# A token model's attention loop: values in tiles of 32 queries, masks in 16 tiles, another order of tasks

## What is computed

```python
Q, K, V = (split_heads(x @ w) for w in (wq, wk, wv))            # 16 heads of 16
local = local_window_attn(Q, K, V)                              # blocks of 64 queries, each sees its block and the one before
GQ = split_heads(x @ wgq)                                       # 8 latent heads of 16
GK, GV = pool_to_latents(x @ wgk), pool_to_latents(x @ wgv)     # 64 latents
lsc = where(latent <= token // chunk, GQ @ GK.T / 4, -inf)
rem = softmax(lsc) @ GV @ r_out_w
gl, gr = sigmoid(Q . gate_local_w), sigmoid(Q . gate_remote_w)
h = h + (gl * local + gr * rem) @ w_out                         # x is the layer norm of h
# then: balanced assignment of all tokens to 8 experts, layer norm, gelu MLP, residual
```

## Time and profile before

| | |
|---|---|
| median of 3 runs | 3000.45 us (2997.2 to 3000.47) |
| profiled execution | 3003.33 us, span 3001.5 us |
| TensorE matmuls busy | 2668.5 us (89%) |
| VectorE busy | 1795.5 us (60%) |
| ScalarE busy | 1091.1 us (36%) |
| GpSimd busy | 752.9 us (25%) |
| granted TensorE clock, mean | 0.971 |

### The profile page before, as it was taken

The page is one execution under the profiler, slowest core; times in us unless marked ns, Lnnn a source line. Parts: engine busy times, 40 slices in busy tenths (PEclk is TensorE's granted clock), DMA queues, the critical chain, the costliest instruction groups (busy, mean ns, idle before and its releaser), DMA issues. The chain is left out here.

```text
span 3001.5 us, 83138 instructions
## 1 busy us (share of the span) xinstructions
PE 2668.5 (89%) x32904; PEld 1793.9 (60%) x32904; DVE 1795.5 (60%) x5503; ACT 1091.1 (36%) x1898; POOL 752.9 (25%) x998
## 2 busy tenths in 40 slices
PE   2899899899999899899899994299999999999998
PEld 1566666666666566566666663166656565666666
DVE  4556556556556556566566556775767667675720
ACT  0343343343343343433333431143333434343343
POOL 1011111121121121121121100134444453434543
PEclk9999999999999999999999998599999999999999
DMA  2000000010010010010000001001020211101020
GB/s 71 11 23 24 17 24 23 17 28 18 17 28 18 18 29 16 19 28 16 21 26 16 23 9 45 15 29 59 30 64 28 65 46 49 64 28 61 30 67 29
DMA packets 51568, 93.71 MB, mean 31 GB/s; under 512 B 7980, under 2 KB 36728, under 8 KB 51096
## 3 DMA queue, kind: packets, MB, share of 16 engines
q0 software_dynamic: 18432, 50.36, 5.9%
q1 hardware_dynamic: 32792, 38.52, 3.9%
HBM read 55.29 MB, written 33.55 MB: 30 GB/s over the span
## 5 line engine op out<-in xcount | busy, mean ns | idle before, releaser
L985 PE MATMUL S_ps<-hT,w 128*128 128x512 f32 x1024 | 478.4, 614 | 15.1 <-ACT hT L694 12.1
L998 PE MATMUL O_ps<-w,hid 128*128 128x256 f32 x2048 | 460.3, 379 | 0.0
L496 POOL DMA_INDIRECT rows<-in_tok_table,idx_now x128 | 129.4, 1011 | 1171.5 <-PE M_ps L883 928.0
L998 PEld LDWEIGHTS O_ps<-w,hid 128*128 128x128 f32 x2048 | 383.0, 190 | 62.5 <-issue 15.3
L1096 DVE TENSOR_REDUCE mxL<-S_ps 128x16 f32<-128x2048 f32 x128 | 293.0, 2289 | 155.8 <-PE S_ps L804 155.8
L632 ACT ACTIVATE PT<-S_ps 128x2048 f32<-128x2048 f32 x128 | 240.3, 1878 | 279.0 <-PE S_ps L772 279.0
L705 ACT ACTIVATE hid<-S_ps,b 128x512 f32<-128x512 f32 x256 | 175.3, 687 | 425.4 <-PE S_ps L985 408.5
L985 PEld LDWEIGHTS S_ps<-hT,w 128*128 128x128 f32 x1024 | 190.0, 194 | 223.5 <-issue 212.1
L828 PEld LDWEIGHTS O_ps<-bdV,PT 128*64 128x64 f32 x7680 | 249.2, 138 | 53.4 <-issue 47.5
L665 ACT ACTIVATE bdV<-M_ps 64x256 f32<-64x256 f32 x256 | 98.8, 386 | 490.7 <-PE M_ps L900 489.2
L828 PE MATMUL O_ps<-bdV,PT 128*64 128x34 f32 x7680 | 263.6, 225 | 1.9 <-DVE loc L1112 1.9
(11 more groups left out here) (237 smaller groups left out, 4248.5 us busy)
## 6 DMA issues: line engine op xcount, KB each, us to landing
h_rows<-h SPq DMA_DIRECT2D x64, 256.0 KB, 2.1
w<-in_w SPq DMA_DIRECT2D x16, 1024.0 KB, 5.9
rows<-in_tok_table,idx_now POOLq DMA_INDIRECT x128, 3.5
out_rows<-orow,idx_cur POOLq DMA_INDIRECT x128, 2.4
PT<-in_tables SPq DMA_DIRECT2D x1, 1024.0 KB
b<-in_b SPq DMA_DIRECT2D x8, 128.0 KB, 4.9
hrow<-h_rows,idx_next POOLq DMA_INDIRECT x64
hrow<-h_rows,idx_cur POOLq DMA_INDIRECT x64
```

The costliest lines, as they stand in the source:

```text
L985: mm = nc.tensor.matmul(S_ps[:, m % 2, 0:GT * P], w1[:, c, m * P:(m + 1) * P], hT[g % 2][:, c, :], start=c == 0, stop=c == KC - 1)
L998: mm = nc.tensor.matmul(O_ps[:, q % 2, 0:D], hid[:, m, q * P:(q + 1) * P], w2[:, m, :], start=m == 0, stop=m == FC - 1)
```

## The change

There are four parts. The values: `pe_values` cuts 64 queries in two halves of 32, so that a weight tile is 128 keys by 32 queries and writes one of four quarters of the partitions of `O_ps`. The masks of S 0 to 5: `pe_small_masks` takes 16 tiles of 32x32, each once, in place of eight matmuls in four tiles of 64x64; the tables are held in two or four rotated copies for it, and are larger in the load and in setup. The masks of S 6 to 9 stay. The order: the four `V` are spread over the rounds S 5 to S 7, `ET` moves to the round of S 8 one iteration sooner (relative sequence 2), the splitting of `mxR` becomes a task of its own (`SPLR`), and `GET`, `G`, `RO`, `ML`, `PK` and `WO 3` change places. The warm-up: iteration -2 does what was written out by hand before.

```diff
+QW = 32
@@ constants
+    turned = lambda a, n: np.stack([np.roll(a, QW * g, 0) for g in range(n)], 1)
-    cols = [..., f(lat), f(np.roll(lat, W, 0)), f(before), f(lane), f(reach), f(lreach), f(pick)]
+    cols = [..., f(turned(lat, NG)), f(before), f(lane), f(turned(reach, 2)), f(turned(lreach, 2)), f(pick)]
@@ ORDER
-            ("ET", 0, 1), ("ET", 1, 1), ("ML", 0, 0), ("OUT", 1, -1), ("RO", 0, -1), ("IDX", 0, 3),
-            ("S", 0, 0), ("G", 0, 1), ("RT", 1, -1), ("POOLX", 0, 1), ("EMB", 0, 2),
-            ("S", 1, 0), ("PK", 0, 1), ("GET", 0, 3), ("Q", 0, 1), ("MT", 0, -1), ("RO", 1, -1), ("EMB", 1, 2),
-            ("S", 2, 0), ("GET", 1, 3), ("K", 0, 1), ("WO", 0, -1), ("WO", 1, -1), ("MT", 1, -1), ("EMB", 2, 2),
-            ("S", 3, 0), ("GET", 2, 3), ("Q", 1, 1), ("PV", 0, 1), ("WO", 2, -1), ("WO", 3, -1), ("EMB", 3, 2),
-            ("S", 4, 0), ("GET", 3, 3), ("K", 1, 1), ("O", 0, 0), ("STATS", 0, 2),
-            ("S", 5, 1), ("O", 1, 0), ("OUT", 0, 0),
-            ("S", 6, 1), ("V", 0, 1), ("V", 1, 1), ("NORM", 0, 2),
-            ("S", 7, 1), ("O", 2, 0),
-            ("S", 8, 1), ("V", 2, 1), ("V", 3, 1), ("RT", 0, 0),
+            ("GET", 3, 2), ("G", 0, 1), ("RO", 0, -1), ("ML", 0, 0), ("OUT", 1, -1), ("IDX", 0, 3),
+            ("S", 0, 0), ("Q", 0, 1), ("RT", 1, -1), ("POOLX", 0, 1), ("EMB", 0, 2),
+            ("S", 1, 0), ("GET", 0, 3), ("K", 0, 1), ("RO", 1, -1), ("MT", 0, -1), ("EMB", 1, 2),
+            ("S", 2, 0), ("WO", 0, -1), ("WO", 1, -1), ("MT", 1, -1), ("PK", 0, 1), ("EMB", 2, 2),
+            ("S", 3, 0), ("GET", 1, 3), ("Q", 1, 1), ("PV", 0, 1), ("WO", 2, -1), ("EMB", 3, 2),
+            ("S", 4, 0), ("GET", 2, 3), ("K", 1, 1), ("WO", 3, -1), ("O", 0, 0), ("STATS", 0, 2),
+            ("S", 5, 1), ("O", 1, 0), ("V", 0, 1), ("OUT", 0, 0),
+            ("S", 6, 1), ("V", 1, 1), ("V", 2, 1), ("SPLR", 0, 1),
+            ("S", 7, 1), ("O", 2, 0), ("V", 3, 1), ("NORM", 0, 2),
+            ("S", 8, 1), ("ET", 0, 2), ("ET", 1, 2), ("RT", 0, 0),
             ("S", 9, 1), ("O", 3, 0), ("SPLIT", 0, 1),
@@ masks of S 0 to S 5
+        def pe_small_masks(pe, into, mask):
+            for n in range(NG):
+                own_ = slice(QW * n, QW * (n + 1))
+                for a in range(NG):
+                    nc.tensor.matmul(into(S_ps[QW * a:QW * (a + 1), n, :]), identb[own_, own_], mask(own_, (n - a) % NG),
+                                     start=True, stop=False)
-                pe_masks(pe, lambda x: x, lambda a, rows_: lreach[rows_:rows_ + W, :])
+                pe_small_masks(pe, lambda x: x, lambda rows_, turn: lreach[rows_, turn % 2, :])
@@ pe_values
-                    for a in range(2):
-                        x = 2 * t + a
+                    for a in range(NG):
+                        x, q = 2 * t + a // 2, QW * (a % 2)
...
-                            weights, vals = PT[:, p, x - back, W * back:W * (back + 1)], bdV[par][:, x - back, p, :, :]
+                            weights, vals = PT[:, p, x - back, W * back + q:W * back + q + QW], bdV[par][:, x - back, p, :, :]
...
-                            weights, vals = PL[:, p - NP, W * x:W * (x + 1)], bdL[par][:, p - NP, :, :]
-                        mm = nc.tensor.matmul(O_ps[W * a:W * (a + 1), t % 2, 2 * OW * p:2 * OW * (p + 1)], weights,
+                            weights, vals = PL[:, p - NP, W * x + q:W * x + q + QW], bdL[par][:, p - NP, :, :]
+                        mm = nc.tensor.matmul(O_ps[QW * a:QW * (a + 1), t % 2, 2 * OW * p:2 * OW * (p + 1)], weights,
@@ waits that follow the order
-                    pe.wait_ge(s_mA, m.out("ET", 1))                # G
+                    pe.wait_ge(s_mA, m.out_before("ET", 1))
-                dve.wait_ge(s_mA, m.out("ET", 1))                   # POOLX
+                dve.wait_ge(s_mA, m.out_before("ET", 1))
-                if m is not None and ("ET", 1) in [x[:2] for x in m.tasks]:   # NORM
-                    dve.wait_ge(s_misc, m.done("ET", 1))
+                if m.prev:
+                    dve.wait_ge(s_mA, m.out_before("ET", 1))
```

More of the change, by code:

```diff
@@ L79, in constants @@
                 pick[32 * g + PIECES * (2 * c + j):32 * g + PIECES * (2 * c + j + 1), c, j, :] = 1.0
+    turned = lambda a, n: np.stack([np.roll(a, QW * g, 0) for g in range(n)], 1)
     f = lambda a: np.ascontiguousarray(a.reshape(P, -1).astype(np.float32))
-    cols = [f(ident), f(parity), f(own), f(i), f(band), f(lat), f(np.roll(lat, W, 0)), f(before), f(lane), f(reach), f(lreach), f(pick)]
+    cols = [f(ident), f(parity), f(own), f(i), f(band), f(turned(lat, NG)), f(before), f(lane), f(turned(reach, 2)), f(turned(lreach, 2)), f(pick)]
     digit = np.arange(1, RADIX, dtype=np.int64)[None, :] << (32 - BITS * (1 + np.arange(DIGITS, dtype=np.int64)))[:, None]
@@ L124, in tower @@
         band = sb("band", [P, 2, P], BF16)
-        latm = sb("latm", [P, 2, TS, NL], BF16)
+        latm = sb("latm", [P, NG, TS, NL], BF16)
         csum = sb("csum", [P, E])
@@ L221, in tower @@
         mp = sba("mp", [P, TS, P])
-        reach = sba("reach", [P, 2 * W], BF16)
-        lreach = sba("lreach", [P, S], BF16)
+        reach = sba("reach", [P, 2, 2 * W], BF16)
+        lreach = sba("lreach", [P, 2, S], BF16)
         pick = sba("pick", [P, KC + 1, 2 * W], BF16)
@@ L240, in tower @@
         xf, xw, xs = (stage[0:SEQS, 6144 + S * n:6144 + S * (n + 1)] for n in (1, 2, 3))
-        woutT = stage[:, 3072:3072 + KC * D].rearrange("p (c n) -> p c n", c=KC)
-        ones = stage[:, 3584:3584 + P]
+        woutT = stage[:, 3584:3584 + KC * D].rearrange("p (c n) -> p c n", c=KC)
+        ones = stage[:, 6144 + S:6144 + S + P]
         wvs = PL[:, 0, :].rearrange("p (c n) -> p c n", c=KC)
@@ L362, in run @@
         def run(eng, iteration):
+            iteration(-2, 2)
             iteration(-1, 3)
@@ L376, in __init__ @@
                 self.tasks = tasks_of(i)
-                known = [x for j in range(-1, i if isinstance(i, int) else 1) for x in tasks_of(j)]
+                known = [x for j in range(-2, i if isinstance(i, int) else 1) for x in tasks_of(j)]
                 more, every = (0, []) if isinstance(i, int) else (i - 1, tasks_of(1))
@@ L491, in gather_rows @@
             pool.wait_ge(s_idx, bb + 1)
-            if m is not None:
+            if m is not None and m.prev:
                 pool.wait_ge(s_misc, m.done(*m.next_task("GET", t)) - 1)
@@ L498, in gather_rows, with power0 @@
                 bass.IndirectOffsetOnAxis(idx_now[:, par, t:t + 1], 0)).then_inc(s_rows[t], 16)
-        def power0(pool, bb, par, m=None):
+        def power0(pool, bb, par, m):
             pool.wait_ge(s_var0, bb + 1)
@@ L503, in power0 @@
                                     op=ALU.pow).then_inc(s_rs0, 1)
-            if m is not None and m.prev:
+            if ("V", TS - 1) in [x[:2] for x in m.prev]:
                 pool.wait_ge(s_mA, m.out_before("V", TS - 1))
@@ L587, in _ @@
             nc.gpsimd.memset(mixc[:, :, :, :], 0.0).then_inc(s_score, 2)
-            for t in range(TS):
+            for t in range(TS - 1):
                 gather_rows(pool, 0, 0, t)
-            power0(pool, 0, 0)
-            for t in range(TS):
-                gather_rows(pool, 1, 1, t)
             def iteration(i, r):
@@ L758, in pe_scores @@
                 stand(pe)
-                pe_masks(pe, lambda x: x.rearrange("p (b n) -> p b n", n=P),
-                         lambda a, rows_: reach[rows_:rows_ + W, :].unsqueeze(1).to_broadcast([W, NB // 2, P]))
+                pe_small_masks(pe, lambda x: x.rearrange("p (b n) -> p b n", n=P),
+                               lambda rows_, turn: reach[rows_, turn % 2, :].unsqueeze(1).to_broadcast([QW, NB // 2, P]))
                 for later in range(2):
@@ L1089, in dve_item @@
                                             negate=True).then_inc(s_mx, 1)
[L1090 to L1094, removed]
                 else:
@@ L1097, in dve_item @@
                                             AX.X, ALU.max, negate=True).then_inc(s_mx, 1)
+            elif name == "SPLR":
+                dve.wait_ge(s_mx, 5 * b + 1)
+                lat = lambda a: a.rearrange("p g t j -> p t g j")
+                rows_ = mp[:, :, :].rearrange("p t (g x) -> p t g x", x=32)
+                chain(dve, dve_split(dve, [rows_[:, :, :, 2 * KC * PIECES + n:2 * (KC + 1) * PIECES:PIECES] for n in range(PIECES)],
+                                     lat(mxR[:, :, :, :]), lat(restR[:, :, :, :]), base), base)
             elif name == "SPLIT":
@@ L1350, in _ @@
             nc.vector.tensor_copy(band[:, :, :].rearrange("p a k -> p (a k)"), c_band)
[L1351 to L1354, removed]
+            nc.vector.tensor_copy(latm[:, :, :, :].rearrange("p n a k -> p (n a k)"), c_lat)
+            nc.vector.tensor_copy(reach[:, :, :].rearrange("p n k -> p (n k)"), c_reach)
+            nc.vector.tensor_copy(lreach[:, :, :].rearrange("p n k -> p (n k)"), c_lreach)
```

(1 more changed line is left out.)

7 lines of the change are left out of this document (3 added, 4 removed).

## The result

The changed kernel takes 3055.45 us (median of 4, 3051.98 to 3060.6) against 2999.22 (median of 4, 2997.2 to 3000.47) for the kernel before: ratio 1.0186, 95% interval 1.0174 to 1.0198. It is 1.9% slower (1.7 to 2.0) where 3.4% faster was forecast. The profiled execution has a span of 3052.6 us.

The account below looks back on a forecast made before the run. TensorE, busy 89% of the span, was taken as the main bound, with VectorE and ACT floors in some rounds. 31 periods x 3.3 us saved, tail 3 less, setup 3 more: 102 less, 2898 us; range 2840 to 2990.

Parts of the forecast that it names:

- the supply of instructions: Attention loop: PE gets instructions in time for an O of 320 in 1.3 us; no wait in the sum.
- rival (3): Attention loop: instructions come too slowly, 0.5 to 0.7 us for an O, 2925 to 2950 us; chance 13%.
- four tiles side by side give 8 ns: Values O: 32-column tiles take 32 ns a pass, four overlap, so O takes 1.4 us and saves 1.05.
- The speed of the small tiles: Values O: 160 passes at 8 ns take 1.28 us, with transition 1.4 us instead of 2.45.
- Rival (5): Values O: every pass pays one tile's 26.8 ns, O takes 4.4 us, kernel 3225 us; chance 10%.
- The masks: S0 to S5: 16 tiles make a mask 0.36 us instead of 0.56; 1.14 us saved in all.
- the walk over rounds: Attention loop: rounds S0 to S9 priced task by task, old to new; period 50.7 us against 54.02.
- The waits it named: New order: PE waits 0.85 us ahead of S0, 0.5 for MT 0, 0.45 for PK, 0.28 before WO.
- DVE's late reduction of S5: S5's round: WO 3 and STATS keep DVE until 2.9 us after the mask; round 5.35 us instead of 4.4.
- The tail: After the steady loop: four O more or less bare, 3 us less.
- The setup: Before the loop: larger tables cost 2.4 us of load and wider casts about 0.6, 3 us more.

Follow-up runs that it names:

- experiment 3: The kernel before with only the masks of S0 to S5 in 16 tiles (larger tables); 2977.95 us, ratio 0.9925.
- experiment 1: The changed kernel with values back in tiles of 64 queries, new order and masks kept; 3006.82 us, ratio 1.0013 against the kernel before.
- experiment 6: The new order alone, with old masks and values in tiles of 64, larger tables kept; 3034.8 us, ratio 1.0115 against the kernel before.
- experiment 4: The changed kernel with each O cut in two halves put apart and some other tasks moved; 3076.16 us, ratio 1.0255 against the kernel before.

## Why the prediction was wrong

**The step that failed** is the supply of instructions: the forecast's sum takes an O at 1.4 us and puts the wait for its instructions at nothing, and rival (3), "Instructions don't come fast enough", prices it at 0.5 to 0.7 us for an O. Its mechanism is what happened; its size was off. (Its times don't follow from its periods either: 52.5 to 53.3 make 2953 to 2978 us, not 2925 to 2950.) Measured are 120 us of such waits in 30 periods, 4.0 a period. O 0 doesn't stall; O 1 to O 3 take 2.57 us from first to last pass in the mean, 1.2 more than one that runs through. The slow clock behind them comes on top: 34.5 us more at the lower level, which costs about half of that, 17. Together 137 of the 149 us by which the 31 periods missed (102 less forecast, 47 more measured); I did not trace the other 12. Because the price was small, the step before it, "four tiles side by side give 8 ns", could be counted as 1.05 us saved on all four O. Something like it (0.91 to 0.95) was had by O 0 and by a third of the others.

The price had a row. The jump's 4.42 us is the one place in the trace of before where PE waits long for "issue". I used it as the cost of a jump. Taken as the time of a transfer it says 256 instructions in about 4 us, and then an O 1 of 320 in 1.4 can't be had after O 0 has drawn 256 and S5's mask and scores 96. The average gave no warning: a period has 2 x 859 = 1718 PE instructions before, and after it 2 x (859 + 64 for O 0 + 3 x 80 for the others + 48 for the masks) = 2422, in the forecast's 50.7 us 48 per us, which is still under the 68 to 74 that the double stalls show. Bursts decide. Before, an O drew 160 in 2.34 us, the same 68 per us, and nothing stalled.

**The speed of the small tiles** was nearly right, where nothing stalls: 160 passes in 1.38 us where 1.28 was forecast, 8.7 ns a pass, and 1.50 to the next task for 1.4. In each of the four column groups 40 passes follow one another, 35 ns each (forecast 32). The forecast and its rows took all four O for alike. O 0 has 128 passes, but its busier groups have 40 as well, so it takes 1.30 us and, with 0.24 to the next mask, 1.54; before, its 64 passes took the 2.30 us of the others' 80 for the same reason. Rival (5), 26.8 ns for each pass, is refuted: 160 of them would be 4.3 us. With it falls, for tiles side by side, the reading of the Trainium skill's page TensorEngine Tiling (Array Packing), section Instruction Overhead, that a matmul costs about 60 cycles however narrow it is; in one tile the passes of line 931 do take 26.8 ns. The sign that rival gave was right, by another mechanism.

**The masks**: a mask to its next kind is 0.37 us in the new rounds (913.46 to 913.83 above), forecast 0.36; experiment 3 gives 0.98 us a period for 1.14.

**The order**: the walk over rounds was right. It held -0.3 for experiment 1 (measured -0.25) and, within that, +0.8 for the order (experiment 6: +0.85). The waits it named are there: 0.78 us on `peak` for 0.85, 0.65 on `h` for 0.45, 0.24 ahead of WO 2 for 0.28, and DVE's late reduction of S5, which starts 2.84 us after the mask at 913.46, forecast 2.9. In the changed kernel DVE shows it as forecast, with WO 3's residual and STATS before the reduction:
```profile
912.02 0.43 DVE L1193 TENSOR_TENSOR h<-hres,M_ps 128x264 f32<-128x264 f32 x1 [2.03 <-PE M_ps L882]
...
914.04 1.40 DVE L1152 BATCH_NORM_STATS2 st<-hres 128x6 f32<-128x256 f32 x4 [0.48 <-issue]
...
916.30 2.29 DVE L1097 TENSOR_REDUCE mxR<-S_ps 128x32 f32<-128x2048 f32 x1
```
**The tail** was wrong by 14 us (3 less forecast, 11 more measured), half clock in a stretch with new idle time. **The setup**: the first DVE instruction starts at 18.63 us instead of 16.29, 2.3 later as forecast (2.4), but the first exponential of S0 is only 0.4 later: most of it was hidden.

## What to carry to other kernels

Splitting matmuls into smaller tiles shortens them (here 2.45 to 1.50 us where nothing stalls) and doubles their instructions. Count what PE draws per us in the burst, not over the loop, and set it against a wait at a loop's jump, which gives a first idea of what a transfer of instructions takes (4.4 us here; 3.5 to 3.75 lie between two stalls). If a burst goes over it, make small tiles only of those operations that stand behind a long stretch of few instructions (here O 0 and O 3), and leave those that follow one another in wide ones. When a wait is removed, look at which engine is late next, and at what the removal itself costs: in experiment 4 it was DVE, and the cut through O. When you count a task's instructions, count each part of it: O 0 had a fifth fewer than I took it for.

## What the runs showed of the hardware

- PE's instructions come in transfers of 16.4 KB, about 256 instructions. Once PE has used up what it holds, it gets 256 in 3.47 to 3.75 us, 68 to 74 per us, and runs again 1.2 to 1.7 us after the end of a transfer (100 of 103 waits). An O of 320 in 1.38 us ran through in 28 of 87 cases, never as O 1, which has O 0's 256 and S5's 96 ahead of it; O 0 ran through each time.
- Four column groups of 32 run side by side on float32 passes that read the same 128 partitions: 8.7 ns a pass, 160 in 1.38 us, where one tile alone has 26.8 ns a pass.
- Idle time costs twice. After 3.5 us idle within 5.66 us the granted clock was 0.50 for the 2.17 us that followed, and in the tail of experiment 1 the same WO took 3.86 us at the 1.2 GHz level and 2.02 at 2.4.
